# Averaging statistics and the scores' bias row in one rounded product

## The reference

```python
q = Wq @ y + bq                      # (128, 1024) per batch
k = Wk @ y + bk
v = Wv @ x + bv
scores = q_h @ k_h.T / sqrt(128)     # 8 heads of 16 channels: (16, 16) each
attn = softmax(scores)
o = Wo @ (attn @ v) + bo + x
h = (o - mean(o)) / sqrt(var(o) + 1e-5) * gn_w + gn_b   # mean and variance over all 128*1024
```

## Time and profile before

| | us |
|---|---|
| median of 3 runs | 1254.44 |
| lowest, highest | 1254.02, 1255.18 |
| profiled execution, device time | 1253.11 |
| profiled execution, span from first to last instruction | 1251.3 |
| TensorE busy | 1239.6 (99%) |
| VectorE busy | 843.2 (67%) |
| ScalarE busy | 807.7 (65%) |
| GpSimd busy | 295.0 (24%) |

### The profile page before, as it was taken

One profiled execution on the slowest core, in us unless ns is written; L12 is line 12 of the kernel. 1 busy time (PEld: TensorE's weight loads), 2 busy tenths in 40 slices (PEclk: granted clock), 3 DMA queues, 4 the chain that ended last, 5 costly groups with the idle time before them and its releaser, 6 DMA issues.

```text
span 1251.3 us, 24584 instructions
## 1 busy us (share of the span) xinstructions
PE 1239.6 (99%) x7860; PEld 968.7 (77%) x7860; DVE 843.2 (67%) x1953; ACT 807.7 (65%) x2884; POOL 295.0 (24%) x297
## 2 busy tenths in 40 slices
PE   8999999999999999999999999999999999999999
PEld 6788888888887888888878877677776767677677
DVE  6777777777747767767667776776665677766554
ACT  6676776666617887887577877655555577755441
POOL 4444443222233233233333305100000111000000
PEclk9999999999999999999999999999999999999999
DMA  9689899999755445554555559998788999888872
GB/s 329 230 289 290 284 289 336 308 309 311 271 189 167 152 152 175 178 172 152 169 166 181 177 177 333 284 270 239 234 243 236 270 255 257 234 225 244 235 222 85
DMA packets 196590, 291.49 MB, mean 233 GB/s; under 512 B 14160, under 2 KB 119888, under 8 KB 195760
## 3 DMA queue, kind: packets, MB, share of 16 engines
q1 hardware_dynamic: 196464, 289.92, 74.5%
HBM read 183.96 MB, written 105.91 MB: 232 GB/s over the span
## 4 chain that ended last, share of the span: by engine, by line
PE 93%; DVE 4%; issue 1%; DMA 1%; SPq 0%; ACT 0%; DVEq 0%
PE bank L695 28%; PE bank L728 23%; PE bank L573 14%; PE bank L759 5%; PE bank L812 5%; PE bank L795 5%; PE bank L645 3%; PE bank L558 2%; PE bank L663 2%; DMA lora_raw_q<-in_factors_q 1%; PE bank L678 1%; PE bank L600 1%; PE bank L617 1%; PE bank L547 1%; DVE op L1364 1%
## 5 line engine op out<-in xcount | busy, mean ns | idle before, releaser
L1032 ACT ACTIVATE bank<-bank,negs 128x128 f32<-128x128 f32 x1024 | 353.9, 360 | 119.4 <-DVE negs L1314 118.5
L695 PE MATMUL bank<-hT,wq 128*128 128x512 f32 x1488 | 363.8, 396 | 0.0
L728 PE MATMUL bank<-wo,op 128*128 128x512 f32 (+1 forms) x1356 | 346.1, 393 | 2.0 <-DVE h_blk L1408 1.5
L695 PEld LDWEIGHTS bank<-hT,wq 128*128 128x128 f32 x1488 | 273.4, 188 | 60.8
L728 PEld LDWEIGHTS bank<-wo,op 128*128 128x128 f32 x1356 | 252.0, 188 | 62.9 <-issue 6.2
L1053 ACT ACTIVATE probT<-bank 128x512 f32<-128x512 f32 x256 | 152.6, 606 | 169.1 <-PE bank L795 166.5
L1309 DVE TENSOR_REDUCE maxes<-bank 128x4 f32<-128x512 f32 x256 | 175.1, 684 | 94.0 <-PE bank L759 93.6
L1032 ACT ACTIVATION_READ_ACCUMULATOR bank<-bank,negs 128x1 f32 x1024 | 231.3, 226 | 0.0
L573 PE MATMUL bank<-wkv_hi,yT 128*128 128x512 f32 x512 | 198.1, 415 | 0.7 <-POOL wkv_lo L1579 0.5
L1408 DVE TENSOR_TENSOR h_blk<-bank,h_blk 128x512 f32<-128x512 f32 x111 | 76.3, 687 | 95.5 <-PE bank L728 94.6
L573 PEld LDWEIGHTS bank<-wkv_hi,yT 128*128 128x128 f32 x512 | 96.5, 188 | 19.3 <-issue 1.7
(11 more groups left out here) (148 smaller groups left out, 1659.5 us busy)
## 6 DMA issues: line engine op xcount, KB each, us to landing
q_dram<-q_part SPq DMA_DIRECT2D x96, 512.0 KB, 5.7
q_stack<-q_dram SPq DMA_DIRECT2D x128, 384.0 KB, 4.8
yT_in<-in_ctx_turned SPq DMA_DIRECT2D x32, 512.0 KB, 4.9
y_in<-in_ctx SPq DMA_DIRECT2D x32, 512.0 KB, 7.1
x_in<-in_x SPq DMA_DIRECT2D x32, 512.0 KB, 5.9
h_dram<-h_out SPq DMA_DIRECT2D x32, 512.0 KB, 7.4
h_in<-h_dram SPq DMA_DIRECT2D x32, 512.0 KB, 4.0
h_blk<-h_dram SPq DMA_DIRECT2D x64, 256.0 KB, 5.2
```

Source lines behind the costliest of these rows:

```text
L695: m = pe.matmul(bank(u % 2).rearrange("p (a n) -> p a n", a=2), wq[:, block, part, c, :], hT[(group + 1) % 2][:, :, of, c, :], start=c == ...
L728: mm = pe.matmul(place[:, columns], op_of(pair, m)[:, of, c, :], wo[m][w][:, c, columns], start=fresh and c == 0 and of == 0 and w == 0, s ...
L1032: act.activation(part, part, ACT.Exp, bias=negs[:, n % NEGS, j:j + 1], scale=SCORE1, accum_out=sums[:, score_column(k), g, j:j + 1]).then_ ...
```

## The change

- The scores' bias row no longer comes from a second float32 product. ScalarE (scale_keys) multiplies the keys' weights wkT0 by the sum of y, twice: once in float32 (y_keys) and once rounded (the upper part of `averaged`). GpSimd (lower_keys) subtracts for the lower part. One rounded product with a matrix of 1/128 sums both parts over the partitions for every output partition.
- VectorE rounds the two statistics columns and takes their rest (st_hi, st_lo), into the same tile. stats_product(b) is then one rounded product of 2 x (2 + 128) = 260 columns, which also sums the bias row of batch b + 2; bias_product does that for batches 0 and 1. stats_product moves behind kv chunk 6, var_product behind chunk 7.
- bias_scores(b + 1) on VectorE, two operations from PSUM, adds the row times bq to score_bias in att ahead of the scores. deviation begins with a reduce that adds the two parts of the statistics (stat_sums).
- The order of VectorE's batch changes: behind the second half of rest_yT come rest_mix, bias_scores(b + 1), deviation(b - 1), norm_factors(b - 2). norm_scale moves from there to the next batch, between begin_gram and finish_gram. lower_b("q") moves to the end of batch 1.
- mix shares n1's memory (evacuate_n1 waits for mix_lo), the broadcast bq leaves the first load (128 columns of 773), and bank 7 is freed by st_sum instead of nm.

No loop, tile size or transfer of the second stage changes. The diff, cut; left out are the semaphores' names and small renamings.

```diff
--- before.py
+++ after.py
@@ -99,21 +99,23 @@
                 table[m] = sb(f"{name}_{m}", [P, HID + COLS[m]], dt)
 
         factor_tiles(lora, "lora", F32R, "kv", "o")
-        ones_avg = sb("ones_avg", [P, P])
-        first = sb("first", [P, 6 * P + 5])
-        w0T, wv0, bqk = first[:, 0:3 * P], first[:, 3 * P:4 * P], first[:, 4 * P:6 * P].rearrange("p (a n) -> p a n", a=2)
+        ones_avg = sb("ones_avg", [P, P], F32R)
+        first = sb("first", [P, 5 * P + 5])
+        w0T, wv0, bk_row = first[:, 0:3 * P], first[:, 3 * P:4 * P], first[:, 4 * P:5 * P]
         score_bias = sb("score_bias", [P, P])
-        bq_col, bv_col, bo_col, gnw_col, gnb_col = (first[:, 6 * P + i:6 * P + i + 1] for i in range(5))
-        bq_scaled = sb("bq_scaled", [P, 1])
+        bq_col, bv_col, bo_col, gnw_col, gnb_col = (first[:, 5 * P + i:5 * P + i + 1] for i in range(5))
+        bq_scaled = sb("bq_scaled", [P, 2])
         minus_half = sb("minus_half", [P, 1])
         y_sum = sb("y_sum", [P, 2])
         gram_mixed = sb("gram_mixed", [P, P])
         gram = sb("gram", [P, P])
         t1 = sb("t1", [P, P])
-        s_bq = sb("s_bq", [P, P])
+        y_keys = sb("y_keys", [P, P])
+        averaged = sb("averaged", [P, 2, 2 + P], F32R)
+        stat_sums = sb("stat_sums", [P, 2])
         att = sb("att", [P, P])
         n1 = sb("n1", [P, P])
-        mix = sb("mix", [P, P])
+        mix = n1
         mix_split = sb("mix_split", [P, 2, P], F32R)
         att_stat = sb("att_stat", [P, 4])
         norm = sb("norm", [P, 16])
...
@@ -294,12 +296,14 @@
                 use_small(7, ("prep", unit_of(b - 1)), ("prep_merged", unit_of(b - 1) + 1))
             for name, done in (("gram", "gram"), ("t1", "t1"), ("s", "s_sb"), ("n1", "n1"), ("mix", "xbias")):
                 use_small(6, (name, b), (done, b + 1))
+            if b < 2:
+                use_small(7, ("u", b), ("u_bias", b + 1))
             if b:
-                use_small(7, ("st", b - 1), ("nm", b))
+                use_small(7, ("st", b - 1), ("st_sum", b))
             if b - 1 >= LATE_STATS:
                 use_small(7, ("var", b - 1), ("ve", b))
         use_small(6, ("kT", B - 1), ("kT", B))
-        use_small(7, ("st", B - 1), ("nm", B))
+        use_small(7, ("st", B - 1), ("st_sum", B))
         use_small(7, ("var", B - 1), ("ve", B))
         for n, place in ((N_UNITS - 2, 7), (N_UNITS - 1, 6)):
             use_small(place, ("prep", n), ("prep_merged", n + 1))
@@ -526,6 +530,10 @@
         def yT_chunks(half):
             return slice(0, NC) if half is None else slice(4 * half, 4 * half + 4)
 
+        def averages(ps, of):
+
+            return ps[:, 0:2 * (2 + P)].rearrange("p (a n) -> p a n", a=2)[:, :, of]
+
         def tensor_program(pe):
             def small_bank(*key):
                 if key in small_freed:
@@ -582,16 +590,24 @@
 
             def stats_product(b):
 
+                of = slice(0, 2 + P if b + 2 < B else 2)
                 ps = small_bank("st", b)
+                pe.wait_ge(S["st_lo"], b + 1)
+                if b + 2 < B:
+                    pe.wait_ge(S["u_lo"], b + 3)
+                pe.matmul(averages(ps, of), ones_avg[:], averaged[:, :, of], start=True, stop=True).then_inc(S["st1_mm"], 1)
+
+            def bias_product(b):
+                of = slice(2, 2 + P)
+                ps = small_bank("u", b)
                 pe.wait_ge(S["const"], CONST["stats"])
-                pe.wait_ge(S["st"], b + 1)
-                pe.wait_ge(S["st2"], b)
-                pe.matmul(ps[:, 0:2], ones_avg[:], both_st, start=True, stop=True).then_inc(S["st1_mm"], 1)
+                pe.wait_ge(S["u_lo"], b + 1)
+                pe.matmul(averages(ps, of), ones_avg[:], averaged[:, :, of], start=True, stop=True).then_inc(S["u_mm"], 1)
 
             def var_product(b):
                 ps = small_bank("var", b)
                 pe.wait_ge(S["st2"], b + 1)
-                pe.matmul(ps[:, 0:1], ones_avg[:], st2, start=True, stop=True).then_inc(S["st2_mm"], 1)
+                pe.matmul(ps[:, 0:1], f32(ones_avg[:]), st2, start=True, stop=True).then_inc(S["st2_mm"], 1)
 
             def t1_product(b):
                 ps = small_bank("t1", b)
@@ -602,9 +618,7 @@
             def score_product(b):
                 ps = small_bank("s", b)
                 pe.wait_ge(S["t1"], b + 1)
-                pe.matmul(ps[:, 0:P], wqT0, t1[:], start=True, stop=False)
-                pe.wait_ge(S["sbq"], b + 1)
-                pe.matmul(ps[:, 0:P], s_bq[:], wkT0, start=False, stop=True).then_inc(S["s_mm"], 1)
+                pe.matmul(ps[:, 0:P], wqT0, t1[:], start=True, stop=True).then_inc(S["s_mm"], 1)
 
             def n1_product(b):
                 ps = small_bank("n1", b)
@@ -832,6 +846,7 @@
             prep_product(7)
             kv_products(0, (1,))
             score_product(0)
+            bias_product(0)
             kv_products(0, (2, 4, 3))
             kv_products(0, (6, 5))
             n1_product(0)
@@ -849,6 +864,8 @@
                 turn_k(b - 1)
                 kv_products(b, (2,))
                 score_product(b)
+                if b == 1:
+                    bias_product(1)
                 mixed_x(b - 1)
                 kv_products(b, (3,))
                 if last:
@@ -859,13 +876,13 @@
                 if last:
                     turn_h(1)
                 mix_product(b)
+                kv_products(b, (6,))
                 stats_product(b - 1)
-                kv_products(b, (6,))
                 if last:
                     turn_h(2)
+                kv_products(b, (7,))
                 if b - 1 >= LATE_STATS:
                     var_product(b - 1)
-                kv_products(b, (7,))
                 if last:
                     turn_h(3)
 
@@ -967,13 +984,22 @@
                 act.activation(lora["kv"][:, 0:HID] if b else x_hi[:], y_in[b % 2][:], ACT.Copy,
                                accum_out=y_sum[:, b % 2:b % 2 + 1]).then_inc(S["ysum"], 1)
 
-            def scale_bias(b):
-                if b:
-                    act.wait_ge(S["s_mm"], b)
-                else:
+            def scale_keys(b):
+
+                if b >= B:
+                    return
+                if b == 0:
                     act.wait_ge(S["first_in"], DMA)
                 act.wait_ge(S["ysum"], b + 1)
-                act.activation(s_bq[:], bqk[:, 0, :], ACT.Copy, scale=y_sum[:, b % 2:b % 2 + 1]).then_inc(S["sbq"], 1)
+                if b:
+                    act.wait_ge(S["u_lo"], b)
+                act.activation(y_keys[:], wkT0, ACT.Copy, scale=y_sum[:, b % 2:b % 2 + 1]).then_inc(S["u_full"], 1)
+                if b > 2:
+                    act.wait_ge(S["st1_mm"], b - 2)
+                elif b:
+                    act.wait_ge(S["u_mm"], b)
+                act.activation(averaged[:, 0, 2:2 + P], wkT0, ACT.Copy,
+                               scale=y_sum[:, b % 2:b % 2 + 1]).then_inc(S["u_hi"], 1)
 
             def round_mix(b):
                 act.wait_ge(S["mix"], b + 1)
...
@@ -1191,10 +1218,25 @@
                 dve.bn_aggr(mv, bn[:].rearrange("p a b -> p (a b)")).then_inc(S["agg"], 1)
                 dve.wait_ge(S["agg"], b + 1)
                 dve.tensor_scalar(st, mv[:, 0:1], xbias[b % 2], None, ALU.add).then_inc(S["st"], 1)
+                if b:
+                    dve.wait_ge(S["st1_mm"], b)
+                else:
+                    dve.wait_ge(S["const"], CONST["stats"])
+                dve.wait_ge(S["st"], b + 1)
+                dve.wait_ge(S["st2"], b)
+                dve.tensor_scalar(averaged[:, 0, 0:2], both_st, 1.0, None, ALU.mult).then_inc(S["st_hi"], 1)
+                dve.wait_ge(S["st_hi"], b + 1)
+                dve.tensor_tensor(averaged[:, 1, 0:2], both_st, f32(averaged[:, 0, 0:2]), ALU.subtract).then_inc(
+                    S["st_lo"], 1)
 
             def deviation(b):
-                mean = small["st", b][:, 0:1]
+                mean = stat_sums[:, 0:1]
                 dve.wait_ge(S["st1_mm"], b + 1)
+                if b:
+                    dve.wait_ge(S["nm"], b)
+                dve.tensor_reduce(stat_sums[:], averages(small["st", b], slice(0, 2)).rearrange("p a n -> p n a"), AX_X,
+                                  ALU.add).then_inc(S["st_sum"], 1)
+                dve.wait_ge(S["st_sum"], b + 1)
                 dve.tensor_tensor(dev, st, mean, ALU.subtract).then_inc(S["dev"], 1)
                 dve.tensor_tensor(nm[b % 2], xbias[b % 2], mean, ALU.subtract).then_inc(S["nm"], 1)
                 dve.wait_ge(S["dev"], b + 1)
@@ -1203,8 +1245,8 @@
             def norm_factors(b):
 
                 if b < LATE_STATS:
-                    dve.wait_ge(S["st1_mm"], b + 2)
-                    var = small["st", b + 1][:, 1:2]
+                    dve.wait_ge(S["st_sum"], b + 2)
+                    var = stat_sums[:, 1:2]
                 else:
                     dve.wait_ge(S["st2_mm"], b - LATE_STATS + 1)
                     var = small["var", b][:, 0:1]
```

(48 more changed lines are left out.)

27 lines of the change are left out of this document (15 added, 12 removed).

## The result

The changed kernel takes 1268.38 us, the median of 4 runs (1265.33 to 1269.2), against 1254.49 us for the kernel before on the same chip (4 runs, 1254.02 to 1255.18): a ratio of 1.0106, with a 95% interval of 1.0088 to 1.0123. The profiled run is the lowest of the four, 1265.33 us, 12.2 us above the profiled run of before. The interval excludes 1: slower by about 1.1%. Here is the page of after, and under it one line of the page of before: shares by engine of the chain of work that ended last.

A forecast was written before the change was run, and what follows sets the result against it. It took VectorE's loop with the trip to GpSimd, not TensorE, to bound the changed kernel; 7.0 (loop) + 2.4 (start) + 1.7 (end) = 11.1 us gave 1264.2 profiled, 1265 as median. Mechanism's range 1257 to 1270, low end put at 1251.

The forecast's parts named there:

- The loop: First stage, one finish_gram to the next: VectorE with the trip to GpSimd's power sets 10.38 us a batch, against 10.13.
- F: The start of finish_gram on VectorE, from which times in a batch are counted; a number in brackets is the batch.
- the first rival: First stage: TensorE stays the bound and the gain arrives, period 9.85 us, whole time 1247.5 us; chance 0.16.
- The rounded product: Statistics product on TensorE: 260 rounded columns cost 0.13 us; a rival had 0.22, changing nothing; no chance given.
- TensorE alone: First stage: with 0.31 us of TensorE work removed, a batch would take 9.82 us if nothing else came late.
- Start: First batches: lower_b("q") behind bias, deviation and a stall delays the first q product to 37.2, 2.4 us (0 to 3).
- That stays, since all of it comes some 0.3 us later: Start: the stall of yT's halves on VectorE by GpSimd's x_lo, 2.61 instead of 0.68 us, remains, shifted 0.3 us.
- End: Batches 30 and 31: later deviations cost 0.7 and 1 us, 1.7 in all (0.5 to 2.5); variance product waits over 1.5.
- 28 loops at one length: Batches 3 to 30: 28 loops, each 0.25 us longer, make 7.0 us slower (2 to 13).
- GpSimd and SyncE move later at no cost: First stage: x_lo ends at F + 12.12 and SyncE's queue moves some 1.5 us later, costing nothing.
- The third rival: Each batch: GpSimd's new subtraction and VectorE block each other, 0.3 us more, loop 10.7, time 1273 us; chance 0.05.
- From the profiled run to the median: Whole kernel: the median of the runs lies 1.3 us above the profiled run, 1264.2 to 1265.5.

The follow-up runs named there:

- e2: The changed kernel without the -0.5 power on GpSimd, norm_factors writing its operand straight to rstd: 1260.2 us, ratio 1.0042.
- e4: The changed kernel with one of the two bias_scores operations on VectorE left out (lower part of the bias): 1256.41 us, ratio 1.0022.
- e6: The changed kernel with deviation and norm_factors ahead of bias_scores, lower_b("q") early, prep_product later, batch 5's prep_rest ahead of lower_b("o"): 1253.62 us, ratio 0.9997.
- e3: The changed kernel with the statistics product issued three times, two more averaging products a batch on TensorE: 1268.08 us, ratio 1.0106.
- e10: e6 with batch 1's x_lo waiting for batch 0's deviation and the output factor's halves lowered behind prep_rest and attention scaling: 1249.91 us, ratio 0.9973.
- e7: The changed kernel with 18 unread transposes on TensorE ahead of the first q product: 1266.87 us in one run.
- e11: The changed kernel with e1's edit and GpSimd's x_lo of batch 1 waiting for batch 0's deviation: 1262.7 us, ratio 1.0082.
- e1: The changed kernel with lower_b("q") back in its old place ahead of the statistics of batch 0: 1265.61 us, ratio 1.0089.
- e9: The changed kernel with, in batch 5, GpSimd's prep_rest ahead of lower_b("o"): 1268.77 us, ratio 1.0119.

## Why the prediction was right, and where it wasn't

- **The loop** (forecast 10.38 us, measured 10.34) was right in its mechanism and nearly in each term, measured against F: scores evacuated at 2.14 (2.16), L1220 at 5.47 (5.49), rest_mix at 7.52 (7.55), norm_factors done at 9.08 (9.13), power begun at 9.17 (9.20), the next F at 10.34. The new rounding took 0.17 and 0.16, the two bias operations 0.34 and 0.35 and the reduce 0.15, all inside their bounds. The load of L616 was idle 0.60 us where I had 0.8; the loop closed 0.04 earlier, and the rest of the difference wasn't followed up. e2, e4 and e6 took the trip, an operation and the order away, and each shortened the batch; e3 loaded TensorE and didn't lengthen it. This settles the first rival.
- **The rounded product** is one load of about 0.12 us (its neighbour L581 follows at 110.47 the L598 of 110.35), and e3 shows that its price doesn't matter.
- **TensorE alone** at 9.82 stays a lower bound: e6 and e10 run at 9.86. Most of the forecast's 0.31 us of gain was there, hidden under the loop.
- **Start** (forecast +2.4, measured +3.2 at F(2), and another 1.6 behind it). The step that was mis-sized is "That stays, since all of it comes some 0.3 us later": the stall of yT's second half stayed (2.75 us from 32.30), but x_lo began 1.31 us later than in the earlier trace rows, not 0.3, and ended at 34.49, 0.91 us later. It waits for ScalarE's x_hi. There the sum of y began 0.59 us later than before (29.06 against 28.47), and two scalings of the keys now stand between it and n1's evacuation, behind which x_hi comes. ScalarE's rows of after, GpSimd's, VectorE's:
```profile
29.06 1.06 ACT L984 ACTIVATE lora_kv<-y_in 128x1024 fp32r<-128x1024 f32 x1 [0.41 <-DMA y_in<-in_ctx]
...
30.24 0.40 ACT L996 ACTIVATE y_keys<-first,y_sum 128x128 f32<-128x128 f32 x1
...
30.99 1.04 ACT L975 CAST x_hi<-x_in 128x1024 fp32r<-128x1024 f32 x1
```
```profile
31.08 0.41 POOL L1731 TENSOR_TENSOR averaged<-y_keys,averaged 128x128 fp32r<-128x128 f32 x1 [5.15 <-ACT averaged L1001]
32.11 2.38 POOL L1724 TENSOR_TENSOR x_lo<-x_in,x_hi 128x1024 fp32r<-128x1024 f32 x1 [0.62 <-ACT x_hi L975]
```
```profile
31.16 0.34 DVE L1229 TENSOR_TENSOR averaged<-norm,averaged 128x2 fp32r<-128x2 f32 x1
...
32.30 2.75 DVE L1182 TENSOR_TENSOR yT<-yT_in,yT 128x512 fp32r<-128x512 f32 x1
```
  What followed began at 34.96 and ran as summed (34.96 + 2.73 = 37.69), and the product behind lora_q came at 37.85, not 37.2. And a consequence is missing from the sum: after those 2.02 us of idle TensorE the granted clock went to the lower level, 1.2 GHz, for 3.41 us, which e7 prices at 1.5 us. e11 shows nearly the whole term to be the lock and the order of one operation: with both mended F(2) is 0.4 us from before's.
- **End** (forecast 0.7 + 1.0, measured 0.74 + 0.97) was right, though the wait in batch 30 came out at 1.47 us, just under the "over 1.5" that I had named as its sign. TensorE's variance product, in batch 30 and 31:
```profile
340.54 0.35 PE L610 MATMUL bank<-norm,ones_avg 128*128 128x1 f32 x2 [1.47 <-DVE norm L1243]
...
353.45 0.35 PE L610 MATMUL bank<-norm,ones_avg 128*128 128x1 f32 x2 [1.19 <-DVE norm L1243]
```
- **28 loops at one length** was too simple. Of the 6.71 us between F(3) and F(30), 27 x 0.20 = 5.4 are the loop's and 1.3 lie in five longer batches (10.49 to 10.66). One of them has the lock again: VectorE's attention scaling took 0.61 instead of 0.29 us at 86.30, while GpSimd lowered the output factor (84.42 to 86.82). In another VectorE waited 0.26 us more ahead of finish_gram for nothing that the profile shows; e11 has it at the same batch. In a third ScalarE waited 0.22 us for y (at 65.37), a wait that before doesn't have. What the two left over come from wasn't followed up.
- **GpSimd and SyncE move later at no cost** held for x_lo: it ends at F + 12.07 of the batch before, and no load waits for it. For SyncE, which I had priced at nothing in the same sentence, it held in most batches and not in all. Behind 35 us ScalarE never waits for y in before, 0.2 us in after, and up to 2.2 us in one batch of e1 to e4 (see e9). The third rival, the lock in every batch, didn't come, but the margin is thin: the subtraction (L1731) runs from 108.98 to 109.39 and st_hi begins at 109.38. Once, at the start, the two did overlap: in the rows above L1229 took 0.34 us instead of 0.16 and ended with the subtraction.
- **From the profiled run to the median** I allowed 1.3 us; it was 3.1. Under e9 stand two things that can lengthen a run, and which of them did it here stays open. This step gives 1.8 of the 3.4 us by which the median lies above 1265. The profiled run itself was forecast at 1264.2 and came at 1265.33, and some of that closeness is luck: the start cost 2.4 us more than its term (0.8 at F(2), and 1.6 behind it, of which 1.5 are the clock), and 1.0 came back in the second stage, for which I had no term.

## What to carry to other kernels

Follow the loop of the busy engine's slowest partner through a whole round before you shorten that engine's work: what decided here wasn't how many operations came to VectorE, but that two of them stood ahead of the one whose answer takes a trip through another engine. Send such a request first and put the independent work into the trip. And where two engines lock each other out, make the long operation of the one wait for the short, critical ones of the other; an added wait of that kind was worth 1.6 us here, and 4.5 where the lower clock went with it.
